# Which table the last odd block of a mixture of experts adds to

## The reference

```python
logits = x @ gate_weight.T
probs = softmax(logits)
topv, topi = top_k(probs, 8)
...
combine = zeros((T, 32)).at[arange(T)[:, None], topi].add(routing_weights)
def expert_step(acc, xs):
    w_gu, w_d, c_e = xs
    g, u = split(x @ w_gu.T, 2, axis=-1)
    h = silu(g) * u
    return acc + h @ w_d.T * c_e[:, None]
out = scan(expert_step, zeros_like(x), (gate_up_proj, down_proj, combine.T))
x = x + out
```

## Time and profile before

| what | value |
|---|---|
| median of 3 runs | 2181.57 us (2181.05 to 2185.69) |
| the profiled execution's own time | 2178.12 us |
| its span, first to last instruction | 2176.3 us |
| TensorE busy | 2041.6 us (94% of the span) |
| stretch from the last scatter's start to the end of the span | 2153.54 to 2176.3, 22.8 us |

### The profile page before, as it was taken

The page is one execution under the profiler, slowest core; times in us unless marked ns, Lnnn a source line. Parts: engine busy times, 40 slices in busy tenths (PEclk is TensorE's granted clock), DMA queues, the critical chain, the costliest instruction groups (busy, mean ns, idle before and its releaser), DMA issues. The chain is left out here.

```text
span 2176.3 us, 27878 instructions
## 1 busy us (share of the span) xinstructions
PE 2041.6 (94%) x8746; PEld 1374.9 (63%) x8746; DVE 1148.5 (53%) x2682; ACT 797.4 (37%) x1986; POOL 973.2 (45%) x945
## 2 busy tenths in 40 slices
PE   7989999998899999999997999999986999999995
PEld 6856666676577844666665666657764555555552
DVE  4247887366442122455554778758864343444442
ACT  2344434143411100233334443425533444444451
POOL 1255664212374200477767566457302444555552
PEclk9999999999999999999998999999997999999998
DMA  5310001200211100011122000110135999888886
GB/s 192 123 53 19 26 26 39 79 2 1 97 59 39 40 8 0 27 40 54 41 86 72 19 26 26 65 66 1 50 137 167 295 299 324 223 217 216 210 213 165
DMA packets 83391, 209.19 MB, mean 96 GB/s; under 512 B 13728, under 2 KB 39840, under 8 KB 74752
## 3 DMA queue, kind: packets, MB, share of 16 engines
q1 hardware_dynamic: 60528, 153.54, 20.5%
q0 software_dynamic: 21280, 51.38, 11.4%
q10 hardware_dynamic: 1440, 2.49, 0.3%
HBM read 257.95 MB, written 34.36 MB: 134 GB/s over the span
## 5 line engine op out<-in xcount | busy, mean ns | idle before, releaser
L98 PE MATMUL banks<-L1f_w,L1f_xT 128*128 x760 | 263.9, 490 | 2.5 <-issue 1.3
L2667 POOL DMA_INDIRECT moe_sums<-L1f_y,L1f_row x95 | 150.6, 1585 | 220.9 <-DVE L1f_is_who L2536 171.0
L159 POOL TENSOR_TENSOR rstd<-rstd,power 128x1 f32<-128x1 f32 x48 | 28.6, 596 | 407.3 <-DVE rstd L153 407.3
L98 PEld LDWEIGHTS banks<-L1f_w,L1f_xT 128*128 128x128 f32 x760 | 137.7, 191 | 82.0 <-issue 6.7
L2675 POOL DMA_INDIRECT L1f_xg<-moe_rows,L1f_row x95 | 94.1, 991 | 63.3 <-DVE L1f_row L2531 36.5
L2503 DVE SCALAR_TENSOR_TENSOR L1f_z<-banks,L1f_share,L1f_sg 128x192 f32<-128x192 f32 x95 | 39.7, 417 | 145.6 <-ACT L1f_sg L2438 145.5
L461 PE MATMUL banks<-L0x_wn,L0x_qT 128*128 128x512 f32 x256 | 115.1, 593 | 0.8 <-DVE x L531 0.8
L461 PE MATMUL banks<-L1x_wn,L1x_qT 128*128 128x512 f32 x256 | 115.1, 593 | 0.8 <-DVE x L531 0.8
L98 PE MATMUL banks<-L0f_down,L0f_z 128*128 128x512 f32 x256 | 111.1, 592 | 1.5 <-DVE L0f_z L1996 1.5
L98 PE MATMUL banks<-L0f_hT_hi,L0f_ug_hi 128*128 128x512 f32 x256 | 100.7, 393 | 11.4 <-POOL L0f_ug_lo L2066 8.7
L2438 ACT ACTIVATE L1f_sg<-banks 128x192 f32<-128x192 f32 x95 | 31.4, 330 | 204.8 <-PE banks L98 130.5
(11 more groups left out here) (402 smaller groups left out, 5265.8 us busy)
## 6 DMA issues: line engine op xcount, KB each, us to landing
L1f_w<-in_experts SPq DMA_DIRECT2D x95, 1280.0 KB
L1f_laid<-moe_counts SPq DMA_DIRECT2D x59, 512.0 KB
w<-in_L1x_heads SPq DMA_DIRECT2D x16, 704.0 KB, 4.0
w<-in_L0x_heads SPq DMA_DIRECT2D x8, 1216.0 KB, 5.6
w<-in_wug SPq DMA_DIRECT2D x8, 1024.0 KB, 4.8
L0x_craw<-in_ctx SPq DMA_DIRECT2D x96, 64.0 KB, 2.1
L1x_craw<-in_ctx SPq DMA_DIRECT2D x96, 64.0 KB, 2.0
w<-in_L0x_out SPq DMA_DIRECT2D x4, 1280.0 KB, 5.4
```

The costliest lines, as they stand in the source:

```text
L98: ins = pe.e.matmul(out, w, m, start=first and n == 0, stop=last and n == len(pairs) - 1)
L159: pool.e.tensor_tensor(self.rstd[:, i:i + 1], self.rstd[:, i:i + 1], self.power[:, 0:1], ALU.pow).then_inc(self.rstd_set.sem, 1)
L2667: pool.e.indirect_dma_start(self.sums[j % 2][:, :], bass.IndirectOffsetOnAxis(ap=self.row[:, j:j + 1], axis=0), self.y[j % self.NY][:], No ...
```

## The change

The function `table(j)` now says which table a block adds to: the second for odd blocks below 93, the first for all others. So block 93, the last odd one, adds to `moe_sums0`, together with block 92 before it and block 94 behind it. `of_table(t)` lists the blocks of a table, and the counts at which SP reads the tables back are made from it: 46 scatters for `moe_sums1` and 49 for `moe_sums0`, where they were 47 and 48. `table_free` makes each scatter wait for the block before it of the same table. For blocks 0 to 92 this is block j - 2 as before. Block 93 now waits for block 92 and no longer for block 91; block 94 waits for block 93 and no longer for block 92.

```diff
+    def table(self, j):
+        return j % 2 if j < self.BLOCKS - 2 else 0
+
+    def of_table(self, t, end=None):
+
+        return [j for j in range(self.BLOCKS if end is None else end) if self.table(j) == t]
+
     def y_left(self, eng, j):
 
         if j >= 0:
-            eng.wait_ge(self.added[j % 2], 16 * (j // 2 + 1))
+            eng.wait_ge(self.added[self.table(j)], 16 * len(self.of_table(self.table(j), j + 1)))
+
+    def table_free(self, eng, j):
+
+        earlier = self.of_table(self.table(j), j)
+        if earlier:
+            self.y_left(eng, earlier[-1])
...
-        sp.wait_ge(self.added[1], 16 * (self.BLOCKS // 2))
+        sp.wait_ge(self.added[1], 16 * len(self.of_table(1)))
         sp.e.dma_start(self.h[:], self.sums[1][0:TOK, :].rearrange("(i p) n -> p i n", p=P)).then_inc(self.odd_back.sem, 16)
-        sp.wait_ge(self.added[0], 16 * ((self.BLOCKS + 1) // 2))
+        sp.wait_ge(self.added[0], 16 * len(self.of_table(0)))
...
             pool.wait_ge(self.y_set, j + 1)
-            self.y_left(pool, j - 2)
-            pool.e.indirect_dma_start(self.sums[j % 2][:, :], bass.IndirectOffsetOnAxis(ap=self.row[:, j:j + 1], axis=0),
-                                      self.y[j % self.NY][:], None, compute_op=ALU.add).then_inc(self.added[j % 2].sem, 16)
+            self.table_free(pool, j)
+            pool.e.indirect_dma_start(self.sums[self.table(j)][:, :], bass.IndirectOffsetOnAxis(ap=self.row[:, j:j + 1], axis=0),
+                                      self.y[j % self.NY][:], None, compute_op=ALU.add).then_inc(self.added[self.table(j)].sem, 16)
```

More of the change, by code:

```diff
@@ L2155, in __init__ @@
         self.y_made, self.y_set, self.added = (
-            take("mixed", n), take("ctx_set", n), [take(f"added{t}", 16 * ((n + 1 - t) // 2)) for t in range(2)])
+            take("mixed", n), take("ctx_set", n), [take(f"added{t}", 16 * len(self.of_table(t))) for t in range(2)])
         self.lane_set, self.steps_to = take("ffn_scaled", 1), {}
```

## The result

| | before | changed |
|---|---|---|
| median of 20 runs | 2180.07 us (2177.27 to 2185.69) | 2187.38 us (2181.71 to 2190.24) |
| ratio of changed to before | | 1.0030, 95% interval 1.0023 to 1.0037 |
| profiled execution, span | 2176.3 us | 2185.7 us |

The forecast was 2181.0 us and no change that can be measured. The changed kernel is slower by 6.5 us (5.0 to 8.1).

A forecast was written before the change was run, and what follows sets the result against it. The tail behind TensorE was taken as bound by DMA bandwidth. It gains 4.2 us, the chain of three scatters takes 3.6, so 0.6 us off 2181.57 gives 2181.0 us; range 2177.6 to 2184.9.

The forecast's parts named there:

- Where the kernel is bound: Behind TensorE's last work: the tail, 18.25 us, is bound by DMA bandwidth, 386 GB/s with the engines full.
- What the early read removes: In the tail: the odd table's 2.1 MB leave it, a gain of 4.2 us by itself.
- t0: Start of the reads of `moe_sums0` behind the last scatter: 2158.05 before, forecast to move to 2161.7.
- my 13.5 and 15.6: Tail lengths behind t0: 13.5 us the low end by bandwidth, 15.6 us the upper bound with all the loss of now.
- The chain's own cost: On POOL, block 93 waits for 92 and 94 for 93: at least 1.9 us, t0 at least 2159.95.
- I take 1.0 us for block 92: Block 92's scatter beside the early odd-table read: delayed by 1.0 us, landing at 2151.8.
- Above: Upper bound of a scatter's delay beside the read: 9.6 us beside weight loads, scaled by row size to 1.9 us.
- Between: Middle estimates of that delay: 0.65 us with one read row between two scatter rows; 1.0 us from stores beside reads.
- my lower bound: Block 94's scatter took 4.50 us with the odd read issued 0.4 us after its descriptors: delay 0 us.
- The sum: Whole span: the tail gains 4.2 us, the chain of three scatters takes 3.6; end 2175.7, 0.6 us sooner.
- the scatter of 92 is held back behind the whole read: Block 92's scatter waits for SP's 64 rows per engine; 2.8 to 4.4 us slower, 2184.4 to 2186.0 us; chance 0.12.
- the second rival: The rival holding block 92's scatter behind the whole read; far end 2186.0 us, chance 0.12.

## Why the prediction was wrong

- **Where the kernel is bound.** Right. The changed part lies behind TensorE's last work, and the tail is bound by bandwidth: taking the odd table out of it makes it 14.7 to 14.8 us, with and without the chain.
- **What the early read removes.** Right within 0.7 us: I took t0 + 14.0, it was t0 + 14.7, between my 13.5 and 15.6. The gain is 3.5 us and not 4.2.
- **The chain's own cost.** The path was right, the size too small: t0 moved by 3.7 us in the run without the early read. I had 1.9 us as its least, and 2.3 us with the terms of my sum (2146.22 + 3 x 4.6 + 2 x 0.15 = 2160.3). The difference is the restart of POOL, which I put at 0.15 us and which is 0.73 us, twice, and a scatter of 4.96 us where I had 4.6.
- **The step that failed** is "I take 1.0 us for block 92". It was 5.3 us. The bound called "Above", 9.6 us of delay beside weights in rows of 10 KB, was scaled down by the size of the neighbour's rows to 1.9 us; even 1.9 us was too low by more than half. The "Between" rows priced only the second part of the delay: one row of the read between two rows of the scatter is close to what the packets show once the scatter's rows pass. What the prediction had at nothing is the time ahead of the first row: 3.2 us more than alone, while some 31 rows of the read pass on each engine. Block 94's undisturbed 4.50 us, my lower bound, said nothing, since the read's data began as it ended.
- **The sum.** I had 0.6 us faster and the profiles show 5.2 us slower, 5.8 us apart: 4.3 from the scatter of 92 (5.6 us forecast, 9.88 measured), 1.2 from two restarts, 0.7 from the tail, less 0.5 because block 93 was not held up at all (4.52 us, where I had 5.0).
- **The rival** "the scatter of 92 is held back behind the whole read" is close to what happened with 2 MB: 92 landing at 2146.22 + 9.88 = 2156.1 in before's clock (I wrote 2155.6), t0 at 2166.8 (2165.1), end 2181.5 (2179.1 to 2180.7). I gave it 0.12, because the gathers of rows 7 were gone here. A scatter can lose 5 us without them; whether they slowed the one of rows 7, no run shows. Its time was right partly by luck, for its mechanism, nothing until 64 rows per engine have passed, is not what the packets show: the first row comes after half of the read, and with 4 MB the scatter lands while the read still has 9 us to go. The prediction says that this rival decides against the change once two scatters lose 1.6 us together; by its own sum (1.4 us lost, 0.6 us left) it is 2.0.
- By the Trainium skill's page, "DMA: Bandwidth & Descriptors", section "Queues, rings and completion order", an engine changes queue only after a packet of several descriptors, 9 to 17 as a rule. My estimate from it, 0.7 to 1.4 us, was one such packet ahead of the scatter. The trace does not agree: 31 to 32 rows per engine pass ahead of it, and then the queues pass about one row for one.
- The range ended at 2184.9 because the second rival's far end was left out of it. A bound of 9.6 us (8.9 with a restart of 0.73 us taken off) had been read from the trace, and a chance of 0.12 stood against it on an argument, not on a row. The measured 2187.38 us lies beyond even that far end, 2186.0.

## What to carry to other kernels

A bulk read that is moved into idle DMA time is not free if a small dependent transfer starts inside it: here 2 MB doubled the time of a 256 KB scatter-add from 4.5 to 9 or 10 us, though the scatter has an eighth of the read's bytes. Before moving a read ahead, look whether the chain that sets the end has a transfer there, and price that transfer by the slowest landing that the trace shows beside a full queue. Here that landing, 14.2 us, would have been too high a price, but on the safe side. And trading two short chains for one long one costs a restart at each link: the early read gave 3.5 us, and the chain alone took 3.7, of which 1.5 were two restarts.

## What the hardware showed that I had not expected

- A scatter beside a read on another queue is delayed with the read's bytes up to 2 MB (+0.8, +2.4, +4.4 to 5.3 us for 0.5, 1 and 2 MB) and no further (+4.3 us beside 4 MB). Beside 2 MB or more its first row comes 5.2 to 5.4 us behind its start instead of 2.0, after some 32 rows of the read on each engine, and then the two queues pass about one row for one.
- The two waits ahead of an indirect DMA on POOL are not alike: 0.24 to 0.27 us from signal to start if the wait written first is met last, 0.73 us if the second is. Exchanging them may have saved some 2 us while the weights are loaded, which is not shown: from the first scatter to the copy of block 92 it was 470.7, 471.0 and 472.9 us in the three exchanged kernels and 472.7 to 475.3 us in the ten others, and the two ranges meet. It costs 0.46 us where the copy is last. The measured times do not tell the sum from nothing in the kernel before.
- POOL writes the descriptors of a plain 2 MB read in 1.6 us, as long as those of one scatter of 128 rows.
